# Four stages of a transformer block on one core: weight preparation and normalization ahead of the last feed-forward stage are rearranged

## The chip, the cores and the metric

The kernel runs on one core of one Trainium2 chip. The metric is the device time of one execution in microseconds. Five engines work side by side, each with its own in-order stream of instructions, and meet only at semaphores: TensorE (PE in the profile, with its weight loads as PEld), VectorE (DVE), ScalarE (ACT), GpSimd (POOL) and SyncE (SP), which issues the DMAs. TensorE's granted clock has two levels, 1.2 and 2.4 GHz, shown as 0.5 and 1.0 of full speed, or as a mean between them over a stretch.

## The reference

An activation `x` of 4 batches of 512 tokens by 256 features passes four residual stages. Only the last two touch this change:

```python
x = x + attention(layernorm(x), ctx, ctx, mask, ...)   # 16 heads of 16
# last stage
def binarize(w):
    return mean(abs(w), axis=1) * sign(w)
n = layernorm(x)                         # no gamma, no beta
h = gelu(n @ binarize(w1).T + b1)        # w1: 1024 x 256
x = x + h @ binarize(w2).T + b2          # w2: 256 x 1024
```

So the last feed-forward stage needs, from each of two 1 MB weights, the signs, and the row means of the magnitudes (alpha1 with 1024 values, alpha2 with 256).

## The kernel before, in words

`attention_phase` covers the attention stage and the last feed-forward stage in one block. The attention is cut into 8 units (`UNITS`), two for each batch, numbered 0 to 7, and each unit into 16 steps (`st`, `STEPS`). Every engine runs the same loop over `u` from -1 to 8 and `st` from 0 to 15, and the order of the work in it is written out by hand with tests on `u` and `st`. A step `t` goes around the engines: TensorE makes two score tiles of 128 x 512 (`scores`, L2046), VectorE masks them and takes the row extreme (`score_max`, L1824), ScalarE exponentiates (L1730), TensorE transposes (`turn_weights`, L2061) into the two-bank PSUM tiles `PT`, ScalarE copies a rounded high part (L1725), VectorE subtracts it for a low part (L1961), and TensorE multiplies both with the values (`weigh`, L2080). The stages of this ring are skewed: TensorE works on scores t+1, transposes t-2, weights t-4, and VectorE's and ScalarE's second parts on t-3.

After each of three head groups of a unit (`G` counts them, three for each unit) a side chain makes the normalized output: ScalarE's `take` copies it out of PSUM, SP's `take_den` moves the denominators, VectorE's `invert` takes the reciprocal, `store_recip` and `spread_recip` send it through memory to tile `RB`, GpSimd's `scale_o` (L1503) multiplies, ScalarE's `high_o` (L1652) and GpSimd's `low_o` (L1509) split. ScalarE waits in `high_o` in its own stream. `project` (in steps 12 to 15 of the next unit) multiplies with the output weights, and `add_y` adds to `x_res`. One PSUM bank, `MB`, serves all small matmul groups in an order that `spare_uses` lists; each use waits until the one before is released.

The last stage is prepared inside the loop. `load_ffn` (L1410, L1412) loads both weights (1 MB each) into `w_stage`, at step 2 of unit 6. GpSimd's `sign(k)` makes for each of 8 pieces of 128 x 512 the sign tile with three instructions (L1541, L1542, L1545) and then the magnitude in place with a fourth (L1547), six pieces in odd steps 5 to 15 of unit 6 and two in unit 7. Its signs lie where the projection weights and the head tiles were, hence waits for the last key, query and value products and for a store. Batch 0 is normalized in unit 7: `ffn_stats` at step 0, `norm_pool`, `ffn_apply` at step 5, and two `ffn_turn` in steps 7 and 8. Each of these transposes four 128 x 128 blocks on TensorE into `MB` (L2095), is copied high by ScalarE (L1674) and low by VectorE (L1845), all three in the same step number. `sums1` and `sums2` take the magnitudes' means with ones in steps 9 and 11.

From unit 8 on the last stage runs as a stream of 32 tiles (`ffn_step(k)`, k from 0 on, 8 tiles for a batch): TensorE makes hidden tile k, ScalarE does gelu and the high copy (L1667), VectorE the low part (`ffn_low`, L1849), and TensorE output tile k-2. The next batch's statistics come at k % 8 = 1, its normalization at 4 and its turns at 5 and 6. At k % 8 = 2 `ffn_add` multiplies the finished outputs of a batch by alpha2 (L1857) into `fin`, which frees their PSUM banks for the next batch (semaphore `ffin`), and adds `fin` to `x_res` (L1863); `add_b2` on GpSimd (L1552) adds the bias before. In unit 8 VectorE also does `invert(22)` and `invert(23)` (in steps 4 and 7), and ScalarE `high_o(22)` and `high_o(23)` in steps 7 and 10.

Of the kernel before, what the change touches and what calls it, by code (L numbers as in the profile page):

```python
# [15 lines left out]
F32 = mybir.dt.float32  # L16
# [1208 lines left out]
def spare_uses():  # L1225

    out = [("turn", 0), ("turn", 1)]
    for u in range(-1, UNITS + 1):
        nxt = (u + 2) // 2
        if u + 1 < UNITS:  # L1230
            out += [("k", u + 1), ("q", u + 1)]
        if nxt < B:
            out += [("v" if u % 2 else "turn", 2 * nxt), ("v" if u % 2 else "turn", 2 * nxt + 1)]
        if u == UNITS - 1:
            out += [("ft", 0), ("ft", 1), ("a1", 0), ("a2", 0)]
        if u >= 1:
            out += [("y", 2 * (u - 1)), ("y", 2 * (u - 1) + 1)]
    return out


def attention_phase(nc, g, sb, ps):
# [8 lines left out]
    mk_at = (nc.sbuf_base + 31) // 32 * 32  # L1250
# [23 lines left out]
    sg = nc.alloc_sbuf_tensor_at("f1_sign", [P, 2, PIECE], F32, offset=mk_at)  # L1274
# [3 lines left out]
          for q in range(2)]  # L1278
# [24 lines left out]
             "fw", "fpos", "fneg", "fsign", "fmag", "fone", "fa", "fal", "fxn", "ftp", "fth", "ftl", "fhid", "fact", "fhi",  # L1303
# [24 lines left out]

    def turn_bank(n):
        return MB[:, :] if n < 2 else PT[1][:, n % 2, :]  # L1330
# [6 lines left out]
    with nc.Block() as block:  # L1337
        @block.sync
        def _(sp):
# [86 lines left out]
            for u in range(-1, UNITS + 1):  # L1426
                nxt = u // 2 + 1
                for st in range(STEPS):
# [7 lines left out]
                    if st == 2 and u == UNITS - 2:  # L1436
                        load_ffn()
# [34 lines left out]
        def _(pool):  # L1472
# [55 lines left out]
            def sign(k):  # L1528
                j, at = divmod(k * PIECE, 2 * H)
                part = g.w_stage[:, j, at:at + PIECE]  # L1530
                dst = SIGNS[j][:, at:at + PIECE]
                pool.wait_ge(s["fw"], 32)
                if k == 0:
                    pool.wait_ge(s["tt"], 2 * STEPS * (UNITS - 2))
                    pool.wait_ge(s["qb"], UNITS)
                    pool.wait_ge(s["kb"], UNITS)
                    pool.wait_ge(s["vb"], 2 * B)
                if at == 0 and j:
                    pool.wait_ge(s_kst, 32 * UNITS)
                pool.wait_ge(s["fsign"], k)  # L1540
# [23 lines left out]
            for u in range(-1, UNITS + 1):  # L1564
                nxt = u // 2 + 1
                for st in range(STEPS):
# [4 lines left out]
                    if u == UNITS - 2 and st in (5, 7, 9, 11, 13, 15):  # L1571
                        sign(st // 2 - 2)
                    if u == UNITS - 1 and st == 2:
                        norm_pool(pool, nm, B, g.power)
                    if u == UNITS - 1 and st in (4, 6):
                        sign(st // 2 + 4)
                    if u == UNITS - 1 and st == 8:
                        add_b2(0)
                    if u == UNITS and st in (4, 10):
                        norm_pool(pool, nm, B + 1 + st // 8, g.power)  # L1580
                    if u == UNITS and st in (8, 14):
                        add_b2(st // 6)
# [25 lines left out]
            add_b2(3)  # L1608

        @block.scalar  # L1610
        def _(act):
# [63 lines left out]

            def tail_silu(n):
# [11 lines left out]
            def ffn_step(k):  # L1688
# [4 lines left out]
                if k >= 5 and k % HT in (5, 6) and k // HT + 1 < B:  # L1693
                    ffn_turn(2 * (k // HT + 1) + k % HT - 5)

            for u in range(-1, UNITS + 1):
                nxt = u // 2 + 1
                for st in range(STEPS):
# [35 lines left out]
                    if u == UNITS - 1 and st in (7, 8):  # L1734
                        ffn_turn(st - 7)
# [24 lines left out]
        def _(dve):  # L1760
# [66 lines left out]
            def ffn_stats(b):  # L1827
                if b:
                    dve.wait_ge(s["yu"], 4 * b + 4)
# [22 lines left out]
            def ffn_add(b):  # L1852
# [3 lines left out]
                for j in range(2):  # L1856
                    dve.tensor_tensor(fin[:, j], YO[j].rearrange("p (t d) -> p t d", d=D), tiles(alpha2[:, :]), ALU.mult)\  # L1857
                        .then_inc(s["ffin"], 1)
                dve.wait_ge(s["fb2"], b + 1)
# [39 lines left out]
            for u in range(-1, UNITS + 1):  # L1899
                nxt = u // 2 + 1  # L1900
                for st in range(STEPS):
# [71 lines left out]
                    if st == (7 if u == UNITS else 6) and u >= 1:  # L1973
# [4 lines left out]
            for k in range(STEPS, ALL + 3):  # L1978
                if k <= ALL:
                    ffn_step(k)  # L1980
# [3 lines left out]
        def _(pe):  # L1984
# [100 lines left out]
            def ffn_turn(n):  # L2085
                b, c = divmod(n, 2)
                if b == 0:
                    spare("ft", n)
                elif b == 1:
# [51 lines left out]
            def ffn_step(k):  # L2141
                if k < ALL:
                    ffn_hidden(k)
                if k % HT in (5, 6) and k // HT + 1 < B:
# [27 lines left out]
            for u in range(-1, UNITS + 1):  # L2172
                nxt = u // 2 + 1
                for st in range(STEPS):
# [33 lines left out]
                    if u == UNITS - 1:  # L2208
                        if st in (7, 8):
                            ffn_turn(st - 7)  # L2210
# [82 lines left out]
```

## Time and profile before

| what | value |
|---|---|
| median of 3 runs | 1335.86 us (1330.07 to 1337.21) |
| the profiled execution, its own time | 1331.35 us |
| its span in the trace | 1329.6 us, so 1.75 us lie around it |
| PE, DVE, ACT, POOL busy | 88%, 66%, 52%, 29% of the span |
| mean granted clock | 0.953 |

The trace gives each instruction's start and length, and, where an engine stood idle before one, the releasing instruction. Times below are microseconds from the start of the span. Units are told apart by the starts of `score_max`: 64 instructions of line 1824 (32 tiles, and 32 short reads of an accumulator) make a unit. Unit 5 runs from 1067.8 to 1114.9, unit 6 to 1176.4, unit 7 to about 1237.5, and the rest is the last stage.

### The profile page before, as it was taken

How to read it: one execution, taken by the hardware profiler on the slowest of the kernel's cores; microseconds unless marked ns; L12 is line 12 of the kernel's file. 1: busy time of each engine (PE TensorE's matmuls, PEld its weight loads, DVE VectorE, ACT ScalarE, POOL GpSimd, SP SyncE). 2: the span in 40 equal slices, each digit the busy share in tenths (PEclk: the TensorE clock that was granted, in tenths of full speed). 3: DMA queues.
4: the chain of work that ended last, by engine and by line, in shares of the span. 5: the costliest groups of instructions: out<-in, count | busy, mean ns of one | idle time of the engine just before them, and what ended most of it. 6: DMA issues, size and time to landing. Idle time of an engine off the chain costs nothing. (4 is left out here: it accounts for less than half of the span.)

```text
span 1329.6 us, 20495 instructions
## 1 busy us (share of the span) xinstructions
PE 1168.6 (88%) x6928; PEld 1015.2 (76%) x6928; DVE 883.1 (66%) x1667; ACT 693.5 (52%) x1045; POOL 383.7 (29%) x373
## 2 busy tenths in 40 slices
PE   3878759988879979969999989999999999688987
PEld 2666648777768869969999978778788788577876
DVE  6778664656545545635655453999989998675675
ACT  2122214555533334434444233887988988665755
POOL 2400027112141600600500044512522621992130
PEclk9988779998889989989999999999999999898999
DMA  8100001002336243252321023321422323210001
GB/s 291 64 0 0 0 8 64 0 5 68 68 60 150 83 132 95 60 155 95 92 94 68 1 71 96 103 69 47 127 71 64 113 83 99 74 33 5 13 26 43
DMA packets 66853, 92.84 MB, mean 70 GB/s; under 512 B 15440, under 2 KB 32592, under 8 KB 66640
## 3 DMA queue, kind: packets, MB, share of 16 engines
q1 hardware_dynamic: 65152, 89.67, 22.9%
q10 hardware_dynamic: 1616, 2.10, 0.5%
q8 instruction: 46, 0.75, 0.2%
q14 instruction: 39, 0.32, 0.1%
HBM read 80.45 MB, written 11.14 MB: 69 GB/s over the span
## 5 line engine op out<-in xcount | busy, mean ns | idle before, releaser
L1824 DVE CUSTOM_DVE_ANT_0 at_pr<-at_sc,at_mk 128x512 f32<-128x512 f32 x256 | 165.5, 684 | 32.3 <-PE at_sc L2046 31.6
L1730 ACT ACTIVATE at_pr<-at_pr,at_nmx 128x512 f32<-128x512 f32 x256 | 170.3, 716 | 19.2 <-DVE at_nmx L1824 18.6
L1961 DVE TENSOR_TENSOR W_1l<-at_pt,W_1h 128x1024 fp32r<-128x1024 f32 x128 | 155.8, 1217 | 12.3 <-ACT W_1h L1725 12.0
L2061 PE MATMUL at_pt<-ident,at_pr 128*128 128x128 f32 x1024 | 137.1, 278 | 21.7 <-DVE W_1l L1961 21.0
L1725 ACT ACTIVATE W_1h<-at_pt 128x1024 fp32r<-128x1024 f32 x128 | 130.7, 1021 | 41.8 <-PE at_o L2080 39.9
L2061 PEld LDWEIGHTS at_pt<-ident,at_pr 128*128 128x128 f32 x1024 | 116.9, 143 | 45.2 <-issue 20.1
L315 DVE TENSOR_TENSOR moe_ms<-moe_hs,moe_gate 128x512 f32<-128x512 f32 x112 | 86.3, 771 | 90.7 <-ACT moe_hs L282 56.5
L282 ACT ACTIVATE moe_hs<-moe_hid,cols 128x512 f32<-128x512 f32 x128 | 88.0, 688 | 103.8 <-PE moe_hid L167 102.9
L274 ACT ACTIVATE moe_hh<-moe_ms 128x512 fp32r<-128x512 f32 x112 | 70.8, 632 | 133.7 <-DVE moe_ms L315 133.7
L301 DVE TENSOR_TENSOR moe_hl<-moe_ms,moe_hh 128x512 fp32r<-128x512 f32 x112 | 87.2, 779 | 69.1 <-ACT moe_hh L274 69.1
L2080 PE MATMUL at_o<-W_1h,at_vaug 128*128 128x512 f32 x256 | 113.8, 444 | 3.0 <-ACT at_hs L1644 2.2
L2080 PE MATMUL at_o<-W_1l,at_vaug 128*128 128x512 f32 x256 | 102.4, 400 | 0.0
L167 PE MATMUL moe_y<-W_1h,moe_hh 128*128 128x256 f32 x256 | 73.6, 288 | 14.0 <-DVE x_res L1213 13.5
L2046 PE MATMUL at_sc<-at_kp,at_qp 128*128 128x512 f32 x256 | 82.9, 401 | 2.1 <-DVE at_nmx L1824 1.6
L167 PE MATMUL moe_y<-W_0h,moe_hh 128*128 128x256 f32 x256 | 72.8, 284 | 9.7 <-DVE x_res L1213 9.7
L167 PE MATMUL moe_y<-W_1l,moe_hh 128*128 128x256 f32 x256 | 73.5, 287 | 0.0
L167 PE MATMUL moe_y<-W_1h,moe_hl 128*128 128x256 f32 x256 | 73.5, 287 | 0.0
L892 ACT ACTIVATE f_hs<-f_hid,cols 128x512 f32<-128x512 f32 x48 | 33.0, 688 | 77.0 <-PE f_hid L167 60.2
L167 PE MATMUL moe_y<-W_0l,moe_hh 128*128 128x256 f32 x256 | 73.0, 285 | 0.0
L167 PE MATMUL moe_y<-W_0h,moe_hl 128*128 128x256 f32 x256 | 73.0, 285 | 0.0
L968 DVE TENSOR_TENSOR f_hl<-f_hs,f_hh 128x512 fp32r<-128x512 f32 x48 | 38.4, 801 | 51.7 <-ACT f_hh L900 51.1
L167 PEld LDWEIGHTS moe_y<-W_1h,moe_hh 128*128 128x128 f32 x256 | 49.9, 195 | 17.8 <-DVE x_res L1213 11.0
(315 smaller groups left out, 3320.2 us busy)
## 6 DMA issues: line engine op xcount, KB each, us to landing
moe_gate<-expert_weights SPq DMA_DIRECT2D x224, 128.0 KB, 2.9
w_stage<-in_ew SPq DMA_DIRECT2D x8, 1024.0 KB, 6.4
at_kp<-at_heads SPq DMA_DIRECT2D x96, 64.0 KB, 2.7
at_qp<-at_heads SPq DMA_DIRECT2D x96, 64.0 KB, 2.7
w_stage<-in_w SPq DMA_DIRECT2D x4, 1024.0 KB, 9.5
f_gate<-expert_weights SPq DMA_DIRECT2D x32, 128.0 KB, 3.0
w_stage<-in_mask SPq DMA_DIRECT2D x16, 256.0 KB, 3.9
at_rb<-at_recip SPq DMA_DIRECT2D x64, 64.0 KB, 2.0
```

Source lines behind the costliest of these rows:

```text
L167: last = pe.matmul(out, lhs(a, c), rhs(b, c), start=start and n == 0, stop=stop and n == m - 1, skip_group_check=skip)
L274: act.activation(m.h[0][:, prev.t % RING, :], m.ms[:, prev.t % RING, :], ACT.Copy).then_inc(m.hi_gated, 1)
L282: act.activation(m.hs[:, cur.t % 2, :], m.hid[cur.t % 2][:, :], func, bias=bias(cur), scale=1.0 if scale is None else scale(cur)).then_inc ...
L301: dve.tensor_tensor(m.h[1][:, r, :], src, f(m.h[0][:, r, :]), ALU.subtract).then_inc(m.split, 1)
L315: dve.tensor_tensor(m.ms[:, r, :], m.hs[:, cur.t % 2, :], m.gate[:, r, :], ALU.mult)\
L1725: act.activation(PH[0][:, n % 2, :], PT[n % 2][:, :, :].rearrange("p c q -> p (c q)"), ACT.Copy)\
L1730: act.activation(pr_of(t)[:, x, :], pr_of(t)[:, x, :], ACT.Exp, bias=nmx[:, t % 4, x:x + 1], scale=-1.0).then_inc(s["ex"], 1)
L1824: dve.tensor_tensor_reduce(pr_of(t)[:, x, :], SB[x][:, :], mk[u // 2 % 2][:, j, :], -float(HD) ** -0.5, 3.0e38, ALU.add, ALU.min, nmx[:, t ...
L1961: dve.tensor_tensor(PH[1][:, n % 2, :], PT[n % 2][:, :, :].rearrange("p c q -> p (c q)"), f(PH[0][:, n % 2, :]), ALU.subtract).then_inc(s[ ...
L2046: pe.matmul(SB[x][:, :], QP[:, h8, j * P:(j + 1) * P], KP[:, h8 // 2, :], start=True, stop=True)\
L2061: last = pe.transpose(PT[t % 2][:, c, j * P:(j + 1) * P], pr_of(t - i + j // 2)[:, j % 2, kc * P:(kc + 1) * P], g.ident[:, :])
L2080: last = pe.matmul(OB[:, :], w, PH[q][:, t % 2, c * T:(c + 1) * T], start=r == 0 and kc == 0 and q == 0, stop=h8 == GROUPS[k][-1] and kc = ...
```

## The change

- `load_ffn` is issued in unit 5, step 6, in place of unit 6, step 2.
- ScalarE makes each piece's sign with one activation (`ffn_sign`), in steps 6, 8, 11, 12, 13 and 14 of unit 6 and 1 and 2 of unit 7. GpSimd keeps the magnitude alone (`magnitude`), in steps 8, 12, 13, 14 of unit 6 and 3, 4, 6, 8 of unit 7.
- Batches 0 and 1 are both normalized and turned in unit 7: statistics in steps 0 and 3, application in 2 and 5, turns in 3, 4, 7 and 8, all through `MB`. Only batches 2 and 3 are prepared in the stream of tiles.
- The bias b2 is added by GpSimd for batches 0 and 1 (steps 10 and 13 of unit 7) and by VectorE (`ffn_bias`) for batches 2 and 3.
- `ffn_add` is split: `ffn_scale`, which frees the PSUM banks, comes ahead of `ffn_low` in its step. `invert(23)` moves from step 7 to step 8 of unit 8.

```diff
-                    if st == 2 and u == UNITS - 2:
+                    if st == 6 and u == UNITS - 3:
                         load_ffn()
...
-                pool.tensor_scalar(sg[:, 0, :], part, 0.0, 1.0, ALU.is_gt, ALU.mult).then_inc(s["fpos"], 1)
-                pool.tensor_scalar(sg[:, 1, :], part, 0.0, -1.0, ALU.is_lt, ALU.mult).then_inc(s["fneg"], 1)
-                pool.wait_ge(s["fpos"], k + 1)
-                pool.wait_ge(s["fneg"], k + 1)
-                pool.tensor_tensor(dst, sg[:, 0, :], sg[:, 1, :], ALU.add).then_inc(s["fsign"], 1)
                 pool.wait_ge(s["fsign"], k + 1)
-                pool.tensor_tensor(part, part, f(dst), ALU.mult).then_inc(s["fmag"], 1)
+                pool.tensor_tensor(part, part, f(SIGNS[j][:, at:at + PIECE]), ALU.mult).then_inc(s["fmag"], 1)
...
+            def ffn_sign(k):
+                j, at = divmod(k * PIECE, 2 * H)
+                act.wait_ge(s["fw"], 32)
+                if k == 0:
+                    act.wait_ge(s["qb"], UNITS)
+                    act.wait_ge(s["kb"], UNITS)
+                    act.wait_ge(s["vb"], 2 * B)
+                if at == 0 and j:
+                    act.wait_ge(s_kst, 32 * UNITS)
+                act.activation(SIGNS[j][:, at:at + PIECE], g.w_stage[:, j, at:at + PIECE], ACT.Sign).then_inc(s["fsign"], 1)
...
+                    if u == UNITS - 2 and st in (6, 8, 11, 12, 13, 14):
+                        ffn_sign(st // 2 - 3 if st < 11 else st - 9)
+                    if u == UNITS - 1 and st in (1, 2):
+                        ffn_sign(st + 5)
+                    if u == UNITS - 1 and st in (3, 4, 7, 8):
+                        ffn_turn(st - 3 if st < 7 else st - 5)
...
+            def ffn_bias(b):
+                dve.wait_ge(s["fxn"], TT * b + TT)
+                dve.tensor_tensor(x_of4(b), x_of4(b), tiles(g.row("b2_1"), TT), ALU.add).then_inc(s["fb2"], 1)
...
             def ffn_step(k):
+                if k >= HT + 2 and k % HT == 2:
+                    ffn_scale(k // HT - 1)
                 if k:
                     ffn_low(k - 1)
                 b = k // HT + 1
-                if b < B and k % HT == 1:
+                if 2 <= b < B and k % HT == 1:
                     ffn_stats(b)
-                if b < B and k % HT == 4:
+                if 2 <= b < B and k % HT == 4:
                     ffn_apply(b)
-                if b < B and k % HT in (5, 6):
+                    ffn_bias(b)
+                if 2 <= b < B and k % HT in (5, 6):
                     ffn_low_turn(2 * b + k % HT - 5)
...
                     if u == UNITS - 1:
-                        if st == 0:
-                            ffn_stats(0)
-                        if st == 5:
-                            ffn_apply(0)
-                        if st in (7, 8):
-                            ffn_low_turn(st - 7)
+                        if st in (0, 3):
+                            ffn_stats(st // 3)
+                        if st in (2, 5):
+                            ffn_apply(st // 3)
+                        if st in (3, 4, 7, 8):
+                            ffn_low_turn(st - 3 if st < 7 else st - 5)
...
-                    if st == (7 if u == UNITS else 6) and u >= 1:
+                    if st == (8 if u == UNITS else 6) and u >= 1:
                         invert(3 * (u - 1) + 2)
```

## Rows read from the trace of the kernel before

**Rows 1.** Busy time by stretch: units 5, 6, 7, last stage; PE, PEld, DVE, ACT, POOL, clock.

```profile
1067.80:1114.90 47.10, 46.72 (x297) 40.61 (x296) 42.85 (x89) 40.09 (x57) 10.16 (x12) 1.00 0.24 69
1114.90:1176.40 61.50, 48.99 (x273) 41.25 (x272) 41.94 (x87) 40.25 (x57) 45.10 (x34) 0.92 0.28 87
1176.40:1237.50 61.10, 52.69 (x316) 45.15 (x315) 45.41 (x101) 40.21 (x56) 27.02 (x20) 0.94 0.09 23
1237.50:1329.60 92.10, 77.47 (x486) 67.93 (x484) 55.68 (x98) 53.69 (x79) 19.59 (x14) 0.97 0.09 27
```

**Rows 2.** The same of line 1824 alone (DVE), units 5 and 6, each cut after ten steps.

```profile
1067.80:1097.40 29.60, 12.97 (x40) 1.00 0.32 95
1097.40:1114.90 17.50, 7.83 (x24) 1.00 0.10 25
1114.90:1144.40 29.50, 13.05 (x41) 1.00 0.51 159
1144.40:1176.40 32.00, 7.81 (x24) 0.84 0.07 20
```

**Rows 3.** The chain of work that ended last, within unit 6: start, length, what.

```profile
1123.63 7.50 DMA w_stage<-in_w
...
1153.49 1.23 POOL at_hs L1503
```

**Rows 4.** Groups of POOL instructions from 1114.9 to 1200: busy us, mean ns, idle before.

```profile
L1542 POOL TENSOR_SCALAR f_sign<-w_stage 128x512 f32<-128x512 f32 x8 | 15.5, 1936 | 0.0
...
L1545 POOL TENSOR_TENSOR f_s<-f_sign 128x512 fp32r<-128x512 f32 x8 | 10.3, 1290 | 1.2
L1547 POOL TENSOR_TENSOR w_stage<-w_stage,f_s 128x512 f32<-128x512 f32 x8 | 10.3, 1284 | 0.6
```

**Rows 5.** The timeline of SP, unit 5 and then unit 6: start, length, instruction.

```profile
1089.14 0.49 SPq L1385 DMA_DIRECT2D at_recip<-at_rc  x1
1090.83 1.32 SPq L1395 DMA_DIRECT2D at_rb<-at_recip  x2
...
1124.15 0.58 SPq L1385 DMA_DIRECT2D at_recip<-at_rc  x1
1131.33 1.27 SPq L1395 DMA_DIRECT2D at_rb<-at_recip  x3
```

**Rows 6.** The timeline of POOL in unit 5, the low part of group 14.

```profile
1100.39 1.30 POOL L1509 TENSOR_TENSOR at_hl<-at_hs,at_hh 128x512 fp32r<-128x512 f32 x1 [2.85 <-ACT at_hh L1652]
```

**Rows 7.** ScalarE: timeline in unit 5, step 13, and a group of the page.

```profile
1108.07 1.03 ACT L1725 ACTIVATE W_1h<-at_pt 128x1024 fp32r<-128x1024 f32 x1 [1.09 <-PE at_o L2080]
...
L274 ACT ACTIVATE moe_hh<-moe_ms 128x512 fp32r<-128x512 f32 x112 | 70.8, 632 | 133.7 <-DVE moe_ms L315 133.7
```

**Rows 8.** Line 1660 alone: the count and length of its table load.

```profile
L1660 ACT ACT_TABLE_LOAD  x1: 1283/1283/1283, 1239.7 to 1239.7; - x1
```

**Rows 9.** Busy time by stretch in unit 7: steps 5, 6, 7 and 9, columns as in rows 1.

```profile
1195.00:1197.50 2.50, 2.27 (x14) 1.88 (x14) 2.50 (x7) 1.52 (x3) 2.27 (x3) 1.00 0.00 0
1197.50:1202.90 5.40, 2.98 (x19) 2.38 (x18) 3.05 (x8) 4.09 (x6) 2.24 (x2) 1.00 0.09 27
...
1208.40:1212.50 4.10, 3.87 (x14) 3.40 (x15) 2.45 (x7) 1.72 (x3) 0.00 (x0) 0.58 0.00 0
...
1191.10:1195.00 3.90, 2.61 (x15) 1.88 (x14) 3.90 (x10) 3.17 (x5) 3.90 (x3) 1.00 0.00 0
```

**Rows 10.** The timeline of DVE in unit 7, step 7: low part of batch 0's first turn.

```profile
1201.14 0.69 DVE L1845 TENSOR_TENSOR xT_l<-at_m,xT_h 128x512 fp32r<-128x512 f32 x1 [2.35 <-ACT xT_h L1674]
```

**Rows 11.** PE in the last stage: its longest waits by releaser, and its turns as a group.

```profile
PE at_pt L167 <- DVE f_fin L1857: 6.5, 3, 3.8
PE at_pt L167 <- DVE f_hl L1849: 1.3, 2, 0.9
...
L2095 PE MATMUL at_pt<-ident,f_xn 128*128 128x128 f32 x24 | 3.6, 274 | 0.2 <-DVE f_xn L1839 0.2
```

**Rows 12.** The timelines of DVE and POOL around k = 8 of the last stage.

```profile
1262.25 4.18 DVE L1849 TENSOR_TENSOR f_hl<-f_hs,f_hh 128x512 fp32r<-128x512 f32 x2 [1.70 <-ACT f_hh L1667]
...
1263.02 2.86 POOL L1552 TENSOR_TENSOR x_res<-x_res,rows 128x1024 f32<-128x1024 f32 x1
```

More of the change, by code:

```diff
@@ L1234, in spare_uses @@
         if u == UNITS - 1:
-            out += [("ft", 0), ("ft", 1), ("a1", 0), ("a2", 0)]
+            out += [("ft", 0), ("ft", 1), ("ft", 2), ("ft", 3), ("a1", 0), ("a2", 0)]
         if u >= 1:
@@ L1302, in attention_phase @@
              "thid", "tact", "thi", "tlo", "ty", "tadd",
-             "fw", "fpos", "fneg", "fsign", "fmag", "fone", "fa", "fal", "fxn", "ftp", "fth", "ftl", "fhid", "fact", "fhi",
+             "fw", "fsign", "fmag", "fone", "fa", "fal", "fxn", "ftp", "fth", "ftl", "fhid", "fact", "fhi",
              "flo", "fy", "fb2", "ffin", "fout", "stored")
@@ L1327, in xf_of, with x_of4 @@
         return g.xT[q][:, c, at:at + T]
+    def x_of4(b):
+        return g.x_res[:, b * TT:(b + 1) * TT, :]
     def turn_bank(n):
-        return MB[:, :] if n < 2 else PT[1][:, n % 2, :]
+        return MB[:, :] if n < 4 else PT[1][:, n % 2, :]
     YO = [PT[0][:, j, :] for j in range(2)]
@@ L1526, in ones, with magnitude @@
                         pool.memset(f(VAUG[:, slot, :, 0:k, PLACE[r] + 2 * HD:PLACE[r] + 2 * HD + 1]), 1.0).then_inc(s_zero, 1)
-            def sign(k):
+            def magnitude(k):
                 j, at = divmod(k * PIECE, 2 * H)
                 part = g.w_stage[:, j, at:at + PIECE]
[L1531 to L1540, printed above, removed]
-                pool.tensor_scalar(sg[:, 0, :], part, 0.0, 1.0, ALU.is_gt, ALU.mult).then_inc(s["fpos"], 1)
-                pool.tensor_scalar(sg[:, 1, :], part, 0.0, -1.0, ALU.is_lt, ALU.mult).then_inc(s["fneg"], 1)
-                pool.wait_ge(s["fpos"], k + 1)
-                pool.wait_ge(s["fneg"], k + 1)
-                pool.tensor_tensor(dst, sg[:, 0, :], sg[:, 1, :], ALU.add).then_inc(s["fsign"], 1)
                 pool.wait_ge(s["fsign"], k + 1)
-                pool.tensor_tensor(part, part, f(dst), ALU.mult).then_inc(s["fmag"], 1)
+                pool.tensor_tensor(part, part, f(SIGNS[j][:, at:at + PIECE]), ALU.mult).then_inc(s["fmag"], 1)
             def add_b2(b):
@@ L1570, in _ @@
                         low_o(3 * (u - 1))
[L1571 to L1582, printed above, removed]
+                    if u == UNITS - 2 and st in (8, 12, 13, 14):
+                        magnitude(0 if st == 8 else st - 11)
+                    if u == UNITS - 1:
+                        if st in (2, 4):
+                            norm_pool(pool, nm, B + st // 2 - 1, g.power)
+                        if st in (3, 4, 6, 8):
+                            magnitude(st // 2 + 3 if st > 4 else st + 1)
+                        if st in (10, 13):
+                            add_b2(st // 3 - 3)
+                    if u == UNITS and st == 10:
+                        norm_pool(pool, nm, B + 2, g.power)
                     if st == 5:
@@ L1692, in ffn_step @@
                     ffn_gelu(k)
-                if k >= 5 and k % HT in (5, 6) and k // HT + 1 < B:
+                if k > HT and k % HT in (5, 6) and k // HT + 1 < B:
                     ffn_turn(2 * (k // HT + 1) + k % HT - 5)
@@ L1827, in ffn_stats @@
             def ffn_stats(b):
-                if b:
-                    dve.wait_ge(s["yu"], 4 * b + 4)
+                if b == B - 1:
+                    dve.wait_ge(s["yu"], 4 * B)
                 norm_stats(dve, nm, ch, x_of(b))
@@ L1850, in ffn_low, with ffn_scale @@
                     .then_inc(s["flo"], 1)
[L1852 removed]
+            def ffn_bias(b):
+                dve.wait_ge(s["fxn"], TT * b + TT)
+                dve.tensor_tensor(x_of4(b), x_of4(b), tiles(g.row("b2_1"), TT), ALU.add).then_inc(s["fb2"], 1)
+            def ffn_scale(b):
                 dve.wait_ge(s["fy"], HT * b + HT)
@@ L1858, in ffn_add @@
                         .then_inc(s["ffin"], 1)
+            def ffn_add(b):
                 dve.wait_ge(s["fb2"], b + 1)
@@ L1977, in _ @@
             add_y(2 * UNITS - 1)
-            for k in range(STEPS, ALL + 3):
-                if k <= ALL:
-                    ffn_step(k)
+            for k in range(STEPS, ALL + 1):
+                ffn_step(k)
+            ffn_scale(B - 1)
             ffn_add(B - 1)
@@ L2086, in ffn_turn @@
                 b, c = divmod(n, 2)
-                if b == 0:
+                if n < 4:
                     spare("ft", n)
-                elif b == 1:
+                elif b == 2:
                     pe.wait_ge(s["pl"], CORE)
@@ L2143, in ffn_step @@
                     ffn_hidden(k)
-                if k % HT in (5, 6) and k // HT + 1 < B:
+                if k > HT and k % HT in (5, 6) and k // HT + 1 < B:
                     ffn_turn(2 * (k // HT + 1) + k % HT - 5)
@@ L2208, in _ @@
                     if u == UNITS - 1:
-                        if st in (7, 8):
-                            ffn_turn(st - 7)
+                        if st in (3, 4, 7, 8):
+                            ffn_turn(st - 3 if st < 7 else st - 5)
                         if st == 9:
```

5 lines of the change are left out of this document (removed).

## The prediction

> **What bounds the kernel now.** I read the page first: TensorE is 88% busy, so time is lost where it isn't. The page's slices show one dip in the attention's second half and several near the end, so I went on to busy time by stretch, with units cut at the starts of line 1824. Unit 5 takes 47.1 us with TensorE busy 46.7 of them: TensorE bounds it. Unit 6 has fewer matmuls and takes 61.5 us with POOL busy 45.1; unit 7 takes 61.1 [rows 1]. Cutting units 5 and 6 after ten steps places the loss: the first ten steps are alike, 29.6 and 29.5 us, the last six take 17.5 and 32.0 [rows 2]. So 14.5 us are lost at the end of unit 6, part of it at a lower clock (0.84 over the stretch).
>
> The chain of waits says by what: the 7.50 us landing of the weights, then POOL's sign and magnitude instructions one behind the other, up to `scale_o` at 1153.49, for which ScalarE waits in `high_o` [rows 3]. One piece costs POOL 1.93 + 1.94 + 1.29 + 1.28 = 6.44 us (the fourth kind, L1541, is like L1542), eight pieces 51.6 us [rows 4]. Each stands ahead of a `scale_o` or `low_o`; ScalarE, then VectorE, then TensorE stop. A second, smaller cause: the reciprocals' round trip through memory takes 1.69 us from store to the next issue in unit 5, and 7.18 us in unit 6, behind the 2 MB [rows 5].
>
> The last stage takes 92.1 us with TensorE busy 77.5 [rows 1]. The waits that matter there are for the banks that `f_fin` frees, 6.5 us in three waits, the longest 3.8, and 1.3 us for low parts [rows 11].
>
> **The change part by part.**
>
> *Unit 5.* The load's two issues take under 1 us of SP and come behind the key stores; the 2 MB then lie in front of the query stores and group 14's reciprocals. Loaded at about 1082.6, which is when SP is through with step 4, they land about 7.5 us later [rows 3], at 1090, and the reciprocals, stored at 1089.14 [rows 5], come 1 to 3 us later than now. The cover is what POOL idles before it takes up `low_o(14)`, 2.85 us [rows 6]. I take 0; if the whole 7.18 - 1.69 = 5.5 us came, 2.6 us would be left over.
>
> *Unit 6.* POOL's work falls from 6.44 to 1.28 us for a piece, four pieces in this unit, 5.1 us beside 45.1 - 38.6 of other work. That removes the 14.5 us. ScalarE gets six activations of 128 x 512. The nearest row is a copy of this shape, 0.63 us [rows 7]. Steps 6 and 8 lack the `turn` that other even units have there; in steps 12 to 14 ScalarE idles 1.09 us a step [rows 7]; only step 11 has no cover, about 0.2 us. Term: -14.3. Bounds: -13 if every uncovered sign delays the ring, -15 if the first ten steps also gain.
>
> *Unit 7, the turns.* Step 7 with a turn takes 5.4 us where step 6 takes 2.5 [rows 9]. VectorE stands 2.35 us before its low part [rows 10], since in one step number TensorE finishes transposes, weights and scores, then turns, then ScalarE copies, and only then VectorE may go on to the ring's low part. This is 2.9 us for a turn, in the ring, and the two new turns are written the same way, in steps 3 and 4: +5.8. Their statistics (1.8 us of VectorE) fit in that idle time. `MB` is not the cause: each turn's bank is free by then. The second application adds a step like step 5, 3.9 us against 2.5 [rows 9]: +1.4. The two signs in steps 1 and 2, where VectorE runs without a break: +0.3. GpSimd's magnitudes and biases have nothing queued that waits: 27.0 us busy in 61.1 now [rows 1].
>
> *Unit 7, the clock.* After the two stalled steps 7 and 8 the clock is 0.58 over step 9, which takes 4.1 us [rows 9]: 1.6 us over 2.5. Two more stalled steps should bring such a stretch in steps 5 to 6: +1.6, bounds 0 and 3.2 (it comes twice now, once in step 9 and once in step 10). Unit 7 in sum: 5.8 + 1.4 + 0.3 + 1.6 = +9.1.
>
> *Last stage.* Removed from TensorE: 8 of 24 turn matmuls, 3.6 / 3 = 1.2 us [rows 11]. The statistics at k = 1 hold up VectorE's last low part of the attention: 0.5 us. The first change of batch, k = 8 to 12: now waits of 3.8 and 0.9 [rows 11], and one stretch at the lower clock behind them, which I price like step 9's [rows 9], 1.7 us. In it two low parts take 4.18 us where two take 1.3 elsewhere, while POOL adds the bias for 2.86 us [rows 12]. Here the trace shows that instructions with two SBUF inputs on both engines slow each other; the bias is moved away. In the new order the scale waits only for low part and statistics: I come to 1.8 us. But `invert(23)` is a step later and ScalarE stops for `scale_o(23)` in its own stream at k = 10, since low parts 9 and 10 come sooner now: 1.8 us new. The 0.9 stays, since it hangs on group 22's reciprocals, and half of the slow clock, 0.8. So 6.4 becomes 5.3: -1.1. The changes at k = 18 and 26 wait 6.5 - 3.8 = 2.7 now; without a low part (0.68 us) ahead of the scale I take 1.0: -1.7. `ffn_bias` on VectorE, 1.3 us twice, falls into steps 12 and 20 where VectorE has room: 0. Sum: -1.2 - 0.5 - 1.1 - 1.7 = -4.5, bounds -2 and -9 (all waits gone).
>
> The Trainium skill bears on this slowdown: "GPSIMD Engine Reference", Specifications, says that GpSimd's SBUF interfaces are shared with VectorE and contended by VectorE instructions with two SBUF inputs. By that rule magnitudes beside the ring are harmless, since the ring's VectorE instructions read PSUM, and `scale_o` and `low_o` in unit 8 go on colliding; the trace agrees (4.18 us for two, against 1.3).
>
> *The sum:* -14.3 + 9.1 - 4.5 = -9.7. Against the profiled execution's own time, 1331.35 (span 1329.6 and 1.75 around it), this is 1321.7. The median shown is 4.5 us above that execution, which makes 1326.2. Which of these a new median meets I can't tell; I take the middle between execution and median, 1333.6, as the base here and for the rivals: 1324.
>
> **The rivals.**
>
> *The turns come cheap* (-14.3 + 1.7 - 4.5 = -17.1, so 1316.5): if the ring absorbed the turns of steps 3 and 4, and with them the slow clock, unit 7 would pay only 9.1 - 5.8 - 1.6 = 1.7 us. Against it: the turn of step 7 makes a step of 5.4 us [rows 9], and nothing in steps 3 and 4 differs from it in kind. For it: at step 3 the ring is later than at 7 by the application before it.
>
> *The clock and the waits take more* (-4, 1329.6): four stalled steps and denser ScalarE work leave TensorE longer at 1.2 GHz, 3.2 us more than counted, and the last stage gains only 2: -14.3 + 12.3 - 2. For it: unit 7 already has a mean of 0.94.
>
> *A load in the wrong place* (-6, 1327.6): the query stores and reciprocals behind 2 MB cost unit 5 the 2.6 us above and a late `fill_half` another 1. Against it: SP issues that fill some 20 us before its first use.
>
> *Slower, the sign's table:* all of ScalarE's functions in the ring run without a table load; the one at 1239.7, for gelu, takes 1.283 us [rows 8]. If Sign is not in the exponential's set, each of eight signs costs two loads, 8 x 2 x 1.283 = 20.5 us on ScalarE. Steps 12 to 14 hide 0.5 us each beyond the sign, so some 18 us are bare: -9.7 + 18 = +8, 1342. It turns the sign of the result once 10 of the 18 us are bare. The Trainium skill, "ScalarE: Activation LUTs", Table sets: the hidden batching unit, says that tables load as sets and names relu, copy, identity and abs as in every set, not sign. By that rule taken narrowly this rival holds; no run here shows a sign.
>
> **How the numbers follow.** Forecast 0.62, cheap turns 0.12, clock and waits 0.13, load 0.06, table 0.07. The range goes from below the cheap turns (with 3.5 us for the bounds of the last stage) to above the clock case: 1313 to 1332, and leaves out the table; the likeliest case's own range is 1319 to 1329. Half a per cent (6.7 us) is about what a measurement of this kernel can tell from none. Faster by more: most of the forecast, all of the cheap turns, a little of the rest, 0.70. Same: 0.22. Slower: 0.08.
>
> **What would show it.** Right: unit 6 at 47 us, with ScalarE's `at_hh` hardly waiting for POOL; steps 3, 4, 7 and 8 of unit 7 at 5.4 us each with VectorE idle 2.35 before the low parts; a clock below 1.0 in steps 5 and 6; unit 7 near 70; the last stage near 87.6, waits for `f_fin` under 3, ScalarE waiting for `at_hs` at k = 10. Wrong: table loads between signs and exponentials; a unit 5 above 48; unit 7 near 63 (cheap turns); the first change of batch still at 6 us.

## The result, and the profile after

The changed kernel takes 1317.93 us (median of 4 runs, 1314.6 to 1320.14) against 1333.19 for the kernel before (4 runs): the ratio is 0.9871, with a 95% interval of 0.9834 to 0.9908. It is faster by 1.3%. The forecast was 1324: the direction was right, its base was 0.4 us above this measurement of the kernel before, and its gain of 9.7 us was too small (15.3 us between the medians, 12.2 between the profiled executions).

The profiled execution after has a span of 1317.4 us (its own time 1319.14), the one before 1329.6: 12.2 us less. The first look is at busy time by stretch, cut at the same instructions as before (the starts of `score_max`, now line 1823). The stretches are units 0 to 5, unit 6, unit 7 up to the start of its last step, and the rest. Columns are as in rows 1. Of the changed kernel:

```profile
834.50:1115.80 281.30, 272.42 (x1673) 228.78 (x1673) 262.35 (x569) 241.90 (x340) 97.99 (x96) 1.00 0.30 89
1115.80:1161.60 45.80, 44.36 (x273) 37.40 (x272) 41.82 (x87) 42.55 (x63) 15.21 (x16) 1.00 0.25 71
1161.60:1228.60 67.00, 53.56 (x302) 45.61 (x302) 47.06 (x111) 40.36 (x58) 19.75 (x16) 0.90 0.08 21
1228.60:1317.40 88.80, 77.82 (x499) 68.45 (x497) 50.95 (x91) 54.70 (x80) 10.41 (x9) 0.99 0.09 28
```

The same cut of the kernel before:

```profile
833.50:1114.90 281.40, 272.39 (x1674) 228.84 (x1673) 262.34 (x568) 242.01 (x340) 98.19 (x96) 1.00 0.28 82
...
1176.40:1234.60 58.20, 49.79 (x294) 42.46 (x293) 42.97 (x97) 38.15 (x54) 27.02 (x20) 0.94 0.09 24
1234.60:1329.60 95.00, 80.38 (x507) 70.62 (x505) 58.12 (x103) 55.76 (x82) 19.59 (x14) 0.98 0.09 27
```

Unit 6 falls from 61.5 [rows 1] to 45.8, so -15.7. Unit 7 rises from 58.2 to 67.0, so +8.8. The rest falls from 95.0 to 88.8, so -6.2. Units 0 to 5 are equal. The sum is -13.1; the stages ahead of the attention took 1.0 us more in this execution, which the change doesn't touch.

Unit 6 first. The groups of POOL and ScalarE from the start of unit 6 show what is left of the 6.44 us for a piece [rows 4]: a magnitude of 1.29 on POOL and a sign of 0.63 on ScalarE, and no table load between signs, copies and exponentials. Of the changed kernel, POOL (first line) and ACT:

```profile
L1533 POOL TENSOR_TENSOR w_stage<-w_stage,f_s 128x512 f32<-128x512 f32 x8 | 10.3, 1286 | 1.5 <-ACT f_s L1669 1.4
```

```profile
L1669 ACT ACTIVATE f_s<-w_stage 128x512 fp32r<-128x512 f32 x8 | 5.0, 626 | 0.0
```

Now steps 3 to 5 and 7 to 9 of unit 7, as busy time by stretch. A turn's step was 5.4 us before and 5.3 to 5.6 at full clock after. The clock falls within step 4, which takes 7.1 us, and again behind step 8. Compare rows 9:

```profile
1172.80:1178.20 5.40, 2.91 (x18) 2.37 (x18) 4.69 (x16) 3.34 (x5) 2.05 (x3) 1.00 0.16 38
1178.20:1185.30 7.10, 4.48 (x18) 3.46 (x18) 3.03 (x8) 2.85 (x4) 2.93 (x3) 0.76 0.01 1
1185.30:1189.10 3.80, 3.59 (x14) 2.86 (x14) 3.74 (x11) 1.73 (x3) 0.00 (x0) 0.61 0.02 4
...
1191.60:1196.90 5.30, 2.94 (x19) 2.37 (x18) 3.03 (x7) 4.12 (x6) 1.13 (x1) 1.00 0.08 26
1196.90:1202.50 5.60, 2.89 (x18) 2.38 (x18) 3.12 (x8) 2.85 (x4) 4.93 (x4) 1.00 0.00 1
1202.50:1206.40 3.90, 3.70 (x14) 3.25 (x15) 2.44 (x7) 1.80 (x3) 0.00 (x0) 0.59 0.02 4
```

In step 3 the statistics of batch 1 lie inside VectorE's idle time, as reckoned: 2.35 us idle [rows 10] become 0.56. In step 4 nothing fills it, and TensorE's turn comes at the lower clock. The timeline of VectorE, changed kernel:

```profile
1173.95 1.39 DVE L94 BATCH_NORM_STATS2 at_st<-x_res 128x6 f32<-128x256 f32 x4
1175.49 0.38 DVE L97 BATCH_NORM_AGGREGATE at_mv<-at_st 128x2 f32<-128x6 f32 x4
1176.43 0.69 DVE L1844 TENSOR_TENSOR xT_l<-at_m,xT_h 128x512 fp32r<-128x512 f32 x1 [0.56 <-ACT xT_h L1658]
...
1183.54 0.69 DVE L1844 TENSOR_TENSOR xT_l<-at_m,xT_h 128x512 fp32r<-128x512 f32 x1 [4.07 <-ACT xT_h L1658]
```

In the last stage TensorE's waits for `f_fin` fall from 6.5 us in three [rows 11] to 2.1 in two, and a new one stands on ScalarE: 3.69 us in `high_o(23)` at k = 10, where it waits for `scale_o(23)`. First the waits of TensorE from 1230 on, then ScalarE's timeline, both of the changed kernel:

```profile
PE at_pt L167 <- DVE f_hl L1848: 2.7, 3, 1.3
PE at_pt L167 <- DVE f_fin L1860: 2.1, 2, 1.1
```

```profile
1257.87 0.78 ACT L1644 ACTIVATE f_hs<-at_sc,cols,f_alpha 128x512 f32<-128x512 f32 x1 [0.69 <-PE at_sc L167]
1262.33 0.63 ACT L1636 ACTIVATE at_hh<-at_hs 128x512 fp32r<-128x512 f32 x1 [3.69 <-POOL at_hs L1504]
```

### The profile page after: what moved, and what is told of

Same layout as the page of the kernel before. It is cut to its first block and busy times, and to the rows that moved or that the text cites. A ratio compares the mean times of both kernels' runs of the same rounds, so it can differ in the third digit from the quotient of the medians.

```text
span 1317.4 us, 20464 instructions
## 1 busy us (share of the span) xinstructions
PE 1167.9 (89%) x6928; PEld 1014.4 (77%) x6928; DVE 879.4 (67%) x1669; ACT 697.0 (53%) x1053; POOL 337.8 (26%) x347
## 5 line engine op out<-in xcount | busy, mean ns | idle before, releaser
L167 PE MATMUL moe_y<-W_1h,moe_hh 128*128 128x256 f32 x256 | 73.6, 288 | 13.9 <-DVE x_res L1213 13.2
L1504 POOL TENSOR_TENSOR at_hs<-at_hs,at_rb 128x512 f32<-128x512 f32 x24 | 32.0, 1332 | 128.3 <-DMA at_rb<-at_recip 128.3
```

Of the source, the lines that this page charges most:

```text
L167: last = pe.matmul(out, lhs(a, c), rhs(b, c), start=start and n == 0, stop=stop and n == m - 1, skip_group_check=skip)
```

## The experiments

Runs of one kernel differ by up to 15 us. The traces, one of each kernel, suggest that most of that lies ahead of the attention: in the twelve kernels of the table, whose text up to there is the same, the first `score_max` starts between 823.7 and 839.8 us, and units 0 to 5 from there on take 281.3 to 281.5 us. So single parts are read from stretches of the traces, and each kernel also by its time from the first `score_max` to the end, 496.1 us for the kernel before and 482.9 for the changed one. Even there a small difference is not sure: changed and turns skewed have the same text in the rest, and it takes 88.8 and 88.0 us. Each ratio is to runs of the kernel before taken alongside (medians 1330.22 to 1333.52), and "from first `score_max`" is one execution. All times in this table are us:

| kernel | unit 6 | unit 7, 15 steps | rest | from first `score_max` | median | ratio to before, 95% interval |
|---|---|---|---|---|---|---|
| before | 61.5 | 58.2 | 95.0 | 496.1 | 1333.19 | |
| changed | 45.8 | 67.0 | 88.8 | 482.9 | 1317.93 | 0.9871 (0.9834 to 0.9908) |
| signs only | 45.9 | 61.4 | 95.7 | 484.4 | 1316.29 | 0.9872 (0.9835 to 0.9909) |
| load late | 46.7 | 67.3 | 87.7 | 483.0 | 1315.74 | 0.9865 (0.9834 to 0.9896) |
| turns skewed | 45.9 | 55.3 | 88.0 | 470.5 | 1304.40 | 0.9786 (0.9748 to 0.9824) |
| invert at 7 | 45.9 | 67.1 | 86.7 | 481.0 | one run | |
| scale behind low | 45.9 | 67.1 | 89.5 | 484.0 | one run | |
| batch 1 in stream | 45.8 | 60.1 | 91.2 | 478.4 | 1311.37 | 0.9824 (0.9780 to 0.9869) |
| bias 1 in unit 8 | 45.9 | 67.1 | 90.2 | 484.5 | one run | |
| skew, invert, early sums | 45.9 | 55.7 | 86.8 | 469.7 | 1306.35 | 0.9786 (0.9748 to 0.9823) |
| stream, skewed, invert | 45.9 | 50.1 | 89.0 | 466.3 | 1297.20 | 0.9748 (0.9715 to 0.9782) |
| skew, invert, late alphas | 45.9 | 53.7 | 87.2 | 468.1 | 1303.04 | 0.9775 (0.9738 to 0.9812) |

**The signs and the load alone**, on the kernel before; batch 1, the bias and `ffn_add` stay as they were.

```diff
+                    if st == 6 and u == UNITS - 3:
...
+                    if u == UNITS - 2 and st in (8, 12, 13, 14):
+                        magnitude(0 if st == 8 else st - 11)
...
+                    if u == UNITS - 2 and st in (6, 8, 11, 12, 13, 14):
+                        ffn_sign(st // 2 - 3 if st < 11 else st - 9)
```

> The kernel before with only two parts of the change: the load in unit 5, and the signs on ScalarE with GpSimd keeping the magnitude. Batch 1 stays in the stream of the last stage. My theory (GpSimd's queue was unit 6's loss, and the moved turns cost about what the prediction says): unit 6 at 46 us against 61.5, unit 7 at 58 (15 steps) and the last stage as before, so about 15 us faster than before, near 1318, as fast as the whole change or 1 to 3 us faster. Rival (the moved batch is what pays, the signs alone leave a stall): unit 6 above 50 us and 1323 or more.

Unit 6 takes 45.9 us: the whole gain there is this part's. In all it gives 11.7 of the 13.2 us from the first `score_max` on, and its median can't be told from the changed kernel's. From the first `score_max` on it was not faster than the changed kernel, as I had half expected: unit 7 took 61.4 in place of 58, at a mean clock of 0.89. The slow stretches fell on step 6, on the stalled step 8 and on step 10. Steps 6, 7 and 8:

```profile
1184.50:1188.40 3.90, 3.65 (x14) 3.16 (x15) 2.63 (x8) 1.72 (x3) 0.00 (x0) 0.60 0.02 5
1188.40:1193.90 5.50, 3.10 (x19) 2.37 (x17) 3.03 (x6) 4.01 (x6) 1.18 (x1) 0.97 0.07 24
1193.90:1200.70 6.80, 4.12 (x18) 3.16 (x18) 3.08 (x8) 2.85 (x4) 4.89 (x4) 0.75 0.00 0
```

Step 6 took 2.5 us before [rows 9] and has the same work. Why the clock fell there already, behind nothing longer than the application of step 5, stays open.

**The load late**, on the changed kernel.

```diff
-                    if st == 6 and u == UNITS - 3:
+                    if st == 2 and u == UNITS - 2:
                         load_ffn()
```

> The changed kernel with the load back in unit 6, step 2. If the load's place matters (7.2 us between the reciprocals' store and the next issue): group 16's scale comes some 5.5 us later, ScalarE waits in unit 6 and the kernel loses 1 to 4 us against the changed one. If it doesn't, since the weights land at step 5 or 6 just ahead of the first sign: 0 to 0.5 us.

Between the reciprocals' store and the next issue lie again 7.4 us, yet unit 6 takes only 0.9 us more (46.7), and the kernel in all 0.1. SyncE's timeline, load late:

```profile
1124.73 0.58 SPq L1386 DMA_DIRECT2D at_recip<-at_rc  x1
1132.15 1.27 SPq L1396 DMA_DIRECT2D at_rb<-at_recip  x3
```

Group 16's `scale_o` comes 6.0 us later in the unit, about as expected, but it has cover: GpSimd idles 3.3 us before the `low_o` that follows, in place of 8.5, and ScalarE waits for neither. So the expected wait did not come. The load's place is worth 0 to 1 us.

This kernel also has step 4 of unit 7, a turn's step with the same instructions as in the changed kernel, at full clock (load late):

```profile
1178.60:1184.20 5.60, 2.90 (x18) 2.37 (x18) 3.11 (x8) 2.85 (x4) 3.03 (x3) 1.00 0.01 2
```

The step before it takes 5.4 us, and both took 2.3 and 2.5 us in the kernel before. So the two new turns cost 6.1 us at full clock, and the low clock adds 1.6 us to step 4 in the changed kernel.

**The turns skewed**, on the changed kernel: ScalarE's and VectorE's part one step number later.

```diff
+                    if u == UNITS - 1 and st in (4, 5, 8, 9):
+                        ffn_turn(st - 4 if st < 8 else st - 6)
...
-                        if st in (3, 4, 7, 8):
-                            ffn_low_turn(st - 3 if st < 7 else st - 5)
+                        if st in (4, 5, 8, 9):
+                            ffn_low_turn(st - 4 if st < 8 else st - 6)
```

> The changed kernel with ScalarE's and VectorE's part of each of the four turns one step number later (4, 5, 8, 9), ScalarE's between its copy of the transposes and its exponentials. If the steps of 5.4 us come from the three parts standing in one step number: steps 3, 4, 7, 8 fall from 5.4, 7.1, 5.3, 5.6 us to about 3 each, the lower clock behind them goes too, unit 7 (15 steps) from 66.9 to about 52 to 56 us, kernel 10 to 14 us faster than the changed one, near 1305. Rival (the single bank for the turns, or VectorE's extra work, sets these steps): under 3 us faster.

Unit 7 falls from 67.0 to 55.3. Steps 3, 4, 7 and 8 take 4.1, 3.0, 2.4 and 3.4 us (5.4, 7.1, 5.3 and 5.6 in the changed kernel), with the same bank and the same instructions. This is inside the expected 52 to 56 us. VectorE no longer idles before the low part of a turn; its timeline, turns skewed:

```profile
1182.92 0.68 DVE L1823 CUSTOM_DVE_ANT_0 at_pr<-at_sc,at_mk 128x512 f32<-128x512 f32 x1
1183.53 0.08 DVE L1823 DVE_READ_ACCUMULATOR2_ANT at_nmx<- 128x1 f32 x1
1183.53 0.68 DVE L1844 TENSOR_TENSOR xT_l<-at_m,xT_h 128x512 fp32r<-128x512 f32 x1
```

So most of a turn's price is its place, not its work. The 11.7 us that unit 7 gives back are not all the ring's: at full clock the four steps take 21.8 us in the kernel with the load late and 12.8 here, 9.0 less, or 2.2 for a turn. Most of the rest is the low clock, 1.6 us in step 4 and 0.7 in step 10 (7.6 to 6.9 us); step 9 falls from 3.9 at 0.59 to 3.0 at 1.00. The edit also moves ScalarE's part within its step, ahead of the exponentials; the two moves weren't tried apart.

**invert(23) back at step 7**, on the changed kernel.

```diff
-                    if st == (8 if u == UNITS else 6) and u >= 1:
+                    if st == (7 if u == UNITS else 6) and u >= 1:
                         invert(3 * (u - 1) + 2)
```

> The changed kernel with invert(23) back in step 7 of unit 8. If ScalarE's 3.7 us wait at k = 10 comes from the reciprocal being a step later: that wait falls by 1 to 3 us and the last stage by 1 to 2. If the wait is set by group 22's reciprocals anyway (VectorE would then wait for the denominators): no change within 0.5 us.

The rest takes 86.7 in place of 88.8 us, and ScalarE's waits for `scale_o`, 5.1 us in the changed kernel, fall to this one line (waits of ScalarE in the rest, invert at 7):

```profile
ACT at_hh L1636 <- POOL at_hs L1504: 0.9, 1, 0.9
```

So this part of the change costs 2.1 us here; its place in the kernel before was the better one. With all four turns skewed, the two kernels below with `invert(23)` at step 7 have a rest of 86.8 and 87.2 against 88.0, so 1 to 2 us is what is shown.

**The scale behind the low part again**, on the changed kernel.

```diff
             def ffn_step(k):
-                if k >= HT + 2 and k % HT == 2:
-                    ffn_scale(k // HT - 1)
                 if k:
                     ffn_low(k - 1)
...
                 if k >= HT + 2 and k % HT == 2:
+                    ffn_scale(k // HT - 1)
                     ffn_add(k // HT - 1)
```

> The changed kernel with ffn_scale put behind ffn_low again. If the scale's place is what shortened the waits for the banks: the waits for f_fin rise from 2.1 us to about 4 us (0.6 us more at each of the three changes of batch) and the last stage, 88.8 us in the changed kernel from the last score_max on, takes 1.5 to 2 us more. If it was the moved work instead: under 0.5 us more.

TensorE's waits for the banks double, as expected, 0.6 us at each of the first two changes of batch and 1.1 at the third, but the rest takes 89.5 against 88.8 us, 0.7 more and not 1.5 to 2 (waits of TensorE, scale behind low):

```profile
PE at_pt L167 <- DVE f_fin L1860: 4.4, 3, 1.7
PE at_pt L167 <- DVE f_hl L1848: 1.0, 2, 0.6
```

The waits for low parts fall from 2.7 to 1.0. Read step by step (from one gelu to the next), the rest says more than its sum. Step k = 18 takes 3.8 us against 3.2 in the changed kernel, and step k = 26 takes 3.3 against 2.1; first the changed kernel's step k = 26, then this one's:

```profile
1298.50:1300.60 2.10, 2.10 (x14) 1.93 (x15) 2.10 (x5) 1.40 (x2) 0.00 (x0) 1.00 0.00 0
```

```profile
1299.20:1302.40 3.20, 2.18 (x14) 2.03 (x15) 3.20 (x6) 1.39 (x2) 0.00 (x0) 1.00 0.00 0
```

These two steps are 1.8 us longer together. Steps k = 7 and 10 are 1.0 us shorter, and that is not the scale's doing: ScalarE waits there for GpSimd's side chain, 1.39 and 3.69 us in the changed kernel and 0.97 and 3.08 here, and the kernel with the turns skewed, which has the scale ahead, also takes 4.9 us at k = 10 against 5.5. So at k = 10 the scale's place changes nothing, since ScalarE's wait stands over it, and at the other two changes of batch it is worth the 1.5 to 2 us expected.

**Batch 1 back in the stream**, on the changed kernel, with its bias on VectorE.

```diff
-            out += [("ft", 0), ("ft", 1), ("ft", 2), ("ft", 3), ("a1", 0), ("a2", 0)]
+            out += [("ft", 0), ("ft", 1), ("a1", 0), ("a2", 0)]
...
-                        if st in (3, 4, 7, 8):
-                            ffn_turn(st - 3 if st < 7 else st - 5)
+                        if st in (7, 8):
+                            ffn_turn(st - 7)
...
-                if 2 <= b < B and k % HT == 1:
+                if b < B and k % HT == 1:
                     ffn_stats(b)
```

> The changed kernel with batch 1 prepared in the stream of tiles again (statistics at k = 1, application at 4, turns at 5 and 6), its bias on VectorE; the split of ffn_add, invert(23) at 8 and all else kept. Unit 7 should fall to that of the signs alone, 58 to 61.5 us (15 steps, 66.9 in the changed kernel). Theory: of the 6.2 us that the last stage gained, some 3 come from the moved preparation (turns, statistics) and 3 from the split and the bias, so the last stage takes 91 to 92 us and the kernel is 2 to 5 us faster than the changed one. Rival: the last stage falls back to 95 us, and the two are even.

The rest takes 91.2 us, 2.4 more than in the changed kernel, and unit 7 takes 60.1, 6.9 less. From the first `score_max` on this is 478.4 against 482.9: moving batch 1 into unit 7 was a loss of 4.5 us, as expected (2 to 5). The moved batch is worth 2.4 us in the last stage, and of the 6.2 us gained there 3.8 come from the other parts.

**The bias of batch 1 in unit 8**, on the changed kernel.

```diff
-                        if st in (10, 13):
-                            add_b2(st // 3 - 3)
+                        if st == 10:
+                            add_b2(0)
+                    if u == UNITS and st == 8:
+                        add_b2(1)
```

> The changed kernel with GpSimd's bias of batch 1 back at step 8 of unit 8. If GpSimd and VectorE slow each other where both read two SBUF inputs: the low parts, the scale or the additions of VectorE beside it take 1.2 to 2 us in place of 0.6, scale_o(23) comes later, and the last stage takes 1 to 3 us more. If not: the bias takes 2.4 us, VectorE's instructions stay at 0.6 to 0.7, and nothing moves by more than 0.5 us.

The rest takes 90.2 us, 1.4 more. Beside POOL's addition of 2.85 us the low part at 1244.66 takes 2.73 us where it takes 0.62 to 0.69 alone. The 1.36 us of the low part ahead of it is not new: the changed kernel has the same beside `low_o(22)`. The timelines of VectorE and POOL, bias 1 in unit 8:

```profile
1239.96 0.69 DVE L1850 TENSOR_TENSOR f_hl<-f_hs,f_hh 128x512 fp32r<-128x512 f32 x1 [1.18 <-ACT f_hh L1653]
1243.21 1.36 DVE L1850 TENSOR_TENSOR f_hl<-f_hs,f_hh 128x512 fp32r<-128x512 f32 x1 [2.56 <-ACT f_hh L1653]
...
1244.66 2.73 DVE L1850 TENSOR_TENSOR f_hl<-f_hs,f_hh 128x512 fp32r<-128x512 f32 x1
```

```profile
1242.74 1.29 POOL L1510 TENSOR_TENSOR at_hl<-at_hs,at_hh 128x512 fp32r<-128x512 f32 x1 [0.74 <-ACT at_hh L1638]
1243.99 2.85 POOL L1538 TENSOR_TENSOR x_res<-x_res,rows 128x1024 f32<-128x1024 f32 x1
```

The Trainium skill's rule of the shared SBUF interfaces ("GPSIMD Engine Reference", Specifications) holds here with these numbers. `scale_o(23)` came no later, against the expectation: POOL waited 2.0 us for its reciprocals anyway. The low clock of the kernel before comes back too. Steps k = 10 and 11 of the kernel before, of the changed kernel, and with the bias in unit 8:

```profile
1266.50:1275.20 8.70, 5.60 (x26) 5.07 (x27) 7.11 (x16) 3.33 (x5) 4.29 (x4) 0.80 0.18 60
```

```profile
1257.90:1264.70 6.80, 4.48 (x27) 3.82 (x28) 3.95 (x10) 3.08 (x5) 4.62 (x4) 1.00 0.29 96
```

```profile
1247.50:1255.60 8.10, 5.64 (x27) 5.11 (x28) 6.95 (x16) 3.38 (x6) 4.42 (x4) 0.79 0.23 79
```

In the traces of all other kernels but signs only, whose last stage is that of the kernel before, these steps run at 1.00. So this single bias, with the low clock behind it, makes steps k = 9 to 11 longer by 1.9 of the 2.5 us that lie between the kernel before and the changed one there.

**The first sums early**, with the skew and invert(23) at step 7.

```diff
-                        if st == 9:
+                        if st == 1:
                             sums1()
...
-                        if st == 10:
+                        if st == 2:
                             alphas()
```

> The changed kernel with the skewed turns, invert(23) at step 7, and the first sums (sums1) moved from step 9 to step 1 of unit 7, their alphas to step 2, beside VectorE's application, where TensorE has about 1.5 us to spare. Unit 7 (15 steps) 53 to 54 us against 55.3 with the skew alone, last stage 86 to 87, the whole 14 to 17 us faster than the changed kernel. If TensorE's 3.5 us for the sums can't be hidden there: 55 us again.

The rest is as expected, 86.8, unit 7 is not: 55.7. Step 10 gets 4.4 us shorter (2.5 in place of 6.9 at a clock of 0.75), and step 2 takes 8.6 us at a clock of 0.65 in place of 3.8, TensorE busy throughout:

```profile
1172.10:1180.70 8.60, 8.60 (x47) 8.04 (x47) 4.09 (x12) 3.17 (x6) 0.00 (x0) 0.65 0.16 33
```

TensorE's sums can't be hidden there; how much of it is the clock and how much the place isn't separated.

**Batch 1 in the stream, batch 0's turns skewed, invert(23) at 7**, on the kernel with batch 1 back in the stream; the diff shows the skew.

```diff
-                    if u == UNITS - 1 and st in (7, 8):
-                        ffn_turn(st - 7)
+                    if u == UNITS - 1 and st in (8, 9):
+                        ffn_turn(st - 8)
...
-                        if st in (7, 8):
-                            ffn_low_turn(st - 7)
+                        if st in (8, 9):
+                            ffn_low_turn(st - 8)
```

> Batch 1 prepared in the stream (as in the run before), batch 0's two turns skewed by one step on ScalarE and VectorE, invert(23) at step 7. From the first score_max on, the kernel before took 496.1 us, the changed one 482.9, batch 1 in the stream 478.4. If moving batch 1 was a loss only through its unskewed turns: unit 7 (15 steps) near 52, last stage 90 to 91, 469 to 471 in all, even with the skewed turns of both batches (470.5). If moving it is a loss anyway: under 468.

It takes 466.3 us from the first `score_max` on, and the median is 1297.20, ratio 0.9748: the best of all, 2.5% faster than the kernel before. My first theory had it at 469 to 471 and the other, that moving batch 1 is a loss anyway, under 468: the second is what came. The cleanest partner is the next kernel, with both batches in unit 7, all four turns skewed, `invert(23)` at step 7, 468.1 us in all and, like this one, at full clock throughout unit 7; its alphas stand later, which its own section shows to cost nothing. There unit 7 takes 3.5 us more (step 2, the application, 1.3; step 3, with the statistics that no longer lie in idle time, 1.8; step 4, 0.4), and the rest only 1.8 less. So with the unskewed turns gone, moving batch 1 is still a loss, of 1.8 us. Unit 7 and the rest of this kernel, then unit 7 of its partner:

```profile
1155.00:1205.10 50.10, 46.32 (x294) 39.60 (x293) 42.96 (x96) 38.29 (x56) 16.32 (x13) 1.00 0.11 28
1205.10:1294.10 89.00, 78.78 (x507) 69.29 (x506) 55.99 (x106) 55.84 (x82) 11.11 (x11) 0.99 0.09 28
```

```profile
1162.20:1215.90 53.70, 47.23 (x302) 40.62 (x302) 46.54 (x111) 39.80 (x58) 19.90 (x16) 1.00 0.10 26
```

**The alphas behind the low part**, with the skew and invert(23) at step 7.

```diff
-                        if st == 10:
-                            alphas()
-                        if st == 12:
-                            alphas2()
...
+                    if u == UNITS - 1 and st == 10:
+                        alphas()
+                    if u == UNITS - 1 and st == 12:
+                        alphas2()
```

> The changed kernel with all four turns skewed, invert(23) at step 7, and VectorE's two alphas at the end of their steps 10 and 12, behind the ring's low part, in place of ahead of it. If the steps of 7 and 5.6 us at the sums come in part from VectorE standing in its own queue: each step falls by 1 to 2 us, unit 7 (15 steps) from 55.3 to 52 to 54, last stage 86.7, and 466 to 468 from the first score_max on. If TensorE's 3.5 us for each of the sums is all of it: 469.3.

Unit 7 takes 53.7 in place of 55.3 us, which looks like the first theory. It is not: step 10 takes 5.3 us here, and 5.3 as well in the kernel above with the alphas ahead. In the run with the skew alone it took 6.9, at a clock of 0.75. First that step with the skew alone, then the one of the kernel above; step 12 is 5.6 us in all three:

```profile
1200.70:1207.60 6.90, 6.90 (x43) 6.39 (x43) 2.62 (x7) 2.92 (x5) 3.73 (x3) 0.75 0.02 3
```

```profile
1185.10:1190.40 5.30, 5.30 (x43) 5.07 (x43) 2.62 (x7) 2.72 (x5) 1.40 (x2) 1.00 0.03 6
```

TensorE is busy throughout both, so the sums cost TensorE's own time and the clock, and VectorE's queue costs nothing there.

## Why the prediction was right, step by step

- **The base.** The middle between execution and median, 1333.6, met the new median of 1333.19. The prediction had no reason for the middle, so this was luck.
- **Unit 5, the load: 0 taken, 0 measured.** Units 0 to 5 take 281.4 and 281.3 us. Group 14's reciprocals came 2.3 us later after their store (4.0 us to the next issue against 1.69 [rows 5]), and POOL's idle time before `low_o(14)` shrank from 2.85 [rows 6] to 1.08 us: the cover was there, and it is nearly used up.
- **Unit 6: -14.3 taken, -15.7 measured.** The mechanism was right, and the signs alone show it by themselves. The term was 1.4 us too small and the result lies outside its bound of -15, since the first ten steps gained more than it allowed for (29.5 us before [rows 2], 28.1 after).
- **Unit 7, the turns: +5.8 taken.** Right: 6.1 at full clock, by steps 3 and 4 of the kernel with the load late. That the price lies mostly in the place, as argued, is shown by the skew. The application, +1.4, is step 2: 3.8 us against 2.5, so 1.3. The two signs, +0.3, cost nothing: step 1 takes 2.5 us before and after.
- **Unit 7, the clock: +1.6 taken.** In sum unit 7 was 9.1 forecast, 8.8 measured. The clock's part was right in size (1.6 in step 4) but not in place: it was expected in steps 5 and 6, and step 5 lost nothing at 0.61.
- **Last stage: -4.5 taken, -6.2 measured**, outside no bound. Step by step, before against after: the turns and statistics of the moved batch (k = 2, 5, 6) give 2.1, 1.7 taken; the changes at k = 18 and 26 give 0.6 and 1.1, exactly the 1.7 taken; the first change of batch (k = 7 to 12) gives 2.4 where 1.1 was taken. This last term was mis-sized: it left half of the slow clock (0.8 us) in place, and at k = 10 and 11 the clock was 1.00 after, against 0.80 before. The new ScalarE wait at k = 10 was foreseen at 1.8 us and measured at 3.7, so the rest of that term gained more than it was given. Undone one by one, the parts give 2.4 (moved batch), 1.4 (bias of batch 1), 0.7 (scale) and -2.1 (`invert(23)`), 2.4 us in sum: they overlap, and the biases of batches 2 and 3 on VectorE were not undone.
- **The rivals.** Cheap turns: refuted, by the steps of 5.3 to 5.6 us. Table loads: refuted; the list of functions in every set in the Trainium skill ("ScalarE: Activation LUTs", Table sets: the hidden batching unit) doesn't name sign, and on this chip Sign ran between exponentials without a load. Load in a wrong place: refuted, 0 to 1 us. More clock and waits: it did not come; unit 7 took 8.8 us more and not 12.3, and the last stage gained 6.2 and not 2.

What the forecast did not say, though its own terms held it: +9.1 for the moved batch in unit 7 against a share of -1.7 in the last stage meant that this part of the change was a loss. Undone, the kernel is 4.5 us faster; undone and with the remaining turns skewed and `invert(23)` at step 7, it is 16.6 us faster from the first `score_max` on.

## What to carry to other kernels

A hand-ordered pipeline whose engines run at a skew has a place for small chains too: put each link of the chain one step number behind the link before it, since two links in one step make the later engine stand for the whole ring (here 2.9 us for each turn, of which the skew gave back 2.2). When a change bundles a large gain with a reordering, price the reordering by itself. Read small parts in stretches that start at a common instruction, since here most of the difference between executions lay ahead of that instruction.

## What the runs showed of the hardware that I had not expected

- Most of the spread shows in one part of the program: over twelve profiled executions, one of each kernel, the start of the attention stage varied by 16 us (823.7 to 839.8), its six first units by 0.2 us.
- What a stretch of lower clock costs depends on the step it falls on. Step 4 of unit 7 took 7.1 us at 0.76 against 5.5 at 1.00, although TensorE was idle for a third of it. Step 5, where VectorE is busy with an application for nearly the whole step, took 3.8 us at 0.61 and 4.1 at 0.58 (load late) against 3.9 at 1.00 in the kernel before [rows 9]: 0.2 us lost at most. Where the stretch falls was not chance here: the changed kernel, invert at 7, scale behind low and bias 1 in unit 8, which differ little or not at all up to the end of unit 7 and whose attention starts anywhere from 823.7 to 835.3 us, all have it on steps 4, 5, 9 and 10. With the load late, unit 6 ends 0.9 us later and step 4 is spared. What sets the place is not shown.
- Between GpSimd and VectorE the slowdown is strong where both read two SBUF inputs: 2.73 us for a low part of 0.68, and 2.85 us for POOL's addition, which takes 2.35 beside the attention's VectorE work, whose instructions read PSUM. Which of the two starts first matters: in the kernel before at k = 12 the addition began at 1276.45, ahead of the low part, and took its 2.41 us, while the low part, begun at 1276.70, took 2.72 and ended 0.6 us after it.
